# Bilinear sampling: summing over the columns with selector matmuls into quarters of the output partitions, and both weights in one VectorE operation

## The reference, cut to what matters

```python
offsets = lax.conv_general_dilated(x, W, padding='SAME', ...) + b     # 2 numbers per pixel and channel
coords  = off.reshape(bc, -1, 2) + grid                               # one (y, x) per output pixel
c0 = clip(coords[..., 0], 0, w - 1); c1 = clip(coords[..., 1], 0, h - 1)
vals_t = vals_lt + (vals_rt - vals_lt) * f0                           # four gathered neighbours
vals_b = vals_lb + (vals_rb - vals_lb) * f0
mapped = vals_t + (vals_b - vals_t) * f1                              # bilinear value
out = x + mapped
```

## Time and profile before

| | us |
|---|---|
| median of 3 runs | 780.98 (777.89 to 781.43) |
| the profiled execution, its own time | 778.75 |
| its span in the trace | 776.9 |
| PE busy | 642.2 (83%) |
| DVE busy | 680.8 (88%) |
| ACT busy | 534.6 (69%) |
| POOL busy | 453.8 (58%) |

### The profile page before, as it was taken

One profiled execution on the slowest core, in us unless ns is written; L12 is line 12 of the kernel. 1 busy time (PEld: TensorE's weight loads), 2 busy tenths in 40 slices (PEclk: granted clock), 3 DMA queues, 4 the chain that ended last, 5 costly groups with the idle time before them and its releaser, 6 DMA issues.

```text
span 776.9 us, 12483 instructions
## 1 busy us (share of the span) xinstructions
PE 642.2 (83%) x4067; PEld 401.1 (52%) x4067; DVE 680.8 (88%) x958; ACT 534.6 (69%) x660; POOL 453.8 (58%) x282
## 2 busy tenths in 40 slices
PE   7899999999998942686777777777767799999997
PEld 5655547688884310354444444545444553565564
DVE  7899997789976789999889999999999955899997
ACT  2666613789965668677876777868867512899995
POOL 3788873000001165999899999889997911422222
PEclk9999999999999985689897898979987999999999
DMA  2004100440001031000000000000000023100001
GB/s 55 5 12 105 23 1 19 75 96 3 3 3 58 18 80 34 1 1 0 1 0 1 1 0 1 0 1 1 0 2 0 1 52 59 29 0 1 0 0 27
DMA packets 28850, 14.94 MB, mean 19 GB/s; under 512 B 23022, under 2 KB 24942, under 8 KB 28654
## 3 DMA queue, kind: packets, MB, share of 16 engines
q1 hardware_dynamic: 27582, 13.61, 8.2%
q10 hardware_dynamic: 1216, 0.66, 0.4%
HBM read 5.14 MB, written 0.78 MB: 8 GB/s over the span
## 4 chain that ended last, share of the span: by engine, by line
PE 41%; DVE 22%; ACT 6%; issue 6%; POOL 6%; DVEq 0%; POOLq 0%; ACTq 0%
PE ps L572 34%; DVE arena L1374 11%; DVE ps L1042 5%; PE ps L754 4%; POOL arena L1777 4%; PE ps L1007 3%; DVE arena L1042 2%; ACT arena L1725 1%; ACT x L1725 1%; POOL x3t L1777 1%; DVE arena L1317 1%; ACT x1t L1725 1%; DVE arena L1319 1%; POOL xn L1777 1%; ACT arena L1609 0%
## 5 line engine op out<-in xcount | busy, mean ns | idle before, releaser
L572 PE MATMUL ps<-arena 128*64 128x64 f32 (+4 forms) x1944 | 340.6, 341 | 99.1 <-DVE arena L1374 36.3
L572 PEld LDWEIGHTS ps<-arena 128*64 128x64 f32 (+4 forms) x1944 | 138.6, 140 | 216.6 <-issue 83.4
L1777 POOL TENSOR_TENSOR arena<-arena 128x1024 f32<-128x1024 f32 x81 | 188.2, 2335 | 23.4 <-DVE arena L1374 8.5
L1374 DVE TENSOR_TENSOR_SCAN arena<-arena,ps 128x1024 f32<-128x1024 f32 x66 | 150.9, 2287 | 8.6
L1042 DVE TENSOR_TENSOR ps<-arena,ps 128x1024 f32<-128x1024 f32 x75 | 90.9, 1212 | 6.9 <-PE ps L572 6.3
L1758 ACT ACTIVATE arena<-ps,nycol 128x1024 f32<-128x1024 f32 x64 | 70.5, 1101 | 24.9 <-PE ps L572 24.9
L1712 ACT ACTIVATE arena<-arena,a_col 128x1024 f32<-128x1024 f32 x66 | 75.4, 1143 | 16.7 <-DVE arena L1374 16.5
L1894 POOL TENSOR_TENSOR arena<-arena,bmask 128x128 f32<-128x128 f32 x64 | 30.2, 472 | 86.9 <-PE ps L572 75.4
L1374 DVE TENSOR_TENSOR_SCAN arena<-ps,arena 128x1024 f32<-128x1024 f32 x30 | 68.2, 2273 | 4.7 <-POOL arena L1777 4.6
L1609 ACT ACTIVATE arena<-arena 128x256 f32<-128x256 f32 x128 | 60.9, 504 | 11.7 <-DVE arena L1255 7.6
L572 PEld LDWEIGHTS ps<-ident,arena 128*128 128x128 f32 x416 | 58.2, 162 | 15.0 <-issue 6.6
(11 more groups left out here) (206 smaller groups left out, 1178.4 us busy)
## 6 DMA issues: line engine op xcount, KB each, us to landing
arena<-arena SPq DMA_DIRECT2D x54, 64.0 KB
arena<-arena SPq DMA_DIRECT2D x12, 128.0 KB, 3.4
w_conv<-in_c_far SPq DMA_DIRECT2D x1, 1152.0 KB, 5.8
w_conv<-rpb_pad SPq DMA_DIRECT2D x36, 28.0 KB, 1.8
arena<-x SPq DMA_DIRECT2D x12, 64.0 KB, 2.0
arena<-x1t SPq DMA_DIRECT2D x12, 64.0 KB, 2.0
arena<-x3t SPq DMA_DIRECT2D x12, 64.0 KB, 2.0
arena<-arena SPq DMA_DIRECT2D x2, 288.8 KB, 3.7
```

What stands on the lines that cost most here:

```text
L572: return pe.matmul(o, l, r, start=start, stop=stop, **k)
L1374: ve.tensor_tensor_scan(hs_ring[n % RING], decay, add, 0.0, ALU.mult, ALU.add).then_inc(S("scan"), 1)
L1777: return gp.tensor_tensor(o, a, b, ALU.mult)
```

## The change

- `turn4` and the reductions on DVE go. In their place PE sums over the columns: `sum_columns` on PE multiplies a selector (`colsel`, 128 x 32: ones on the 32 partitions of a batch, in that batch's column, zeros elsewhere) with `prod` of each of the 4 groups `t` of a channel step, and writes to partitions 32 t to 32 t + 31 of one bank, 6 + p. Over the eight steps of a half the selector is shifted by one column, and all add up in that one bank, since its other columns are zero. The four matmuls come once for each channel step, 16 times in all. `prod` has 8 buffers in place of 4 so that a whole step can wait.
- After the eighth step of a half, DVE copies the bank (512 wide, `copy_sums`), PE turns it with four transposes (`turn_sums`), and DVE finishes with four small operations that read PSUM (`finish_pair`). For the first half this comes inside step 8 of the loop; POOL finishes nothing any more.
- The hat of y moves from ACT to DVE: `hat4` computes both negated hats in one operation, 1024 wide. ACT keeps the `|d|` alone. The two signs cancel, so `finish` adds where it subtracted.
- PE's loops over the steps are written out; DVE's loop body is two steps long.
- POOL fills `colsel` (a small memset and a copy) before the stage.

```diff
@@ -329,12 +330,13 @@
             pixels = out[b].rearrange("h w c -> (h w) c").rearrange("(k p) c -> p k c", p=P)
             eng.dma_start(pixels[:, blocks], yout[:, blocks, b]).then_inc(S("stored"), 16)
 
-        def finish(eng, p, h):
+        def finish(eng, p, h, b):
+            turned = ps[:, 6 + p, :].rearrange("p (k g a b j) -> p k g a b j", k=4, g=CGRP, a=2, b=2)
             return eng.tensor_tensor(
-                yout[:, 4 * h:4 * h + 4, 2 * p:2 * p + 2].rearrange("p k b (g j) -> p k (b g) j", g=CGRP),
-                x3_row.rearrange("p (k n) -> p k n", k=NBLK)[:, 4 * h:4 * h + 4, DI * p:DI * p + DI]
-                .rearrange("p k (n j) -> p k n j", j=CPER),
-                sampled[:, :, 2 * h:2 * h + 2, :, CPER * p:CPER * p + CPER].rearrange("p k b g j -> p k (b g) j"), ALU.subtract)
+                yout[:, 4 * h:4 * h + 4, 2 * p + b].rearrange("p k (g j) -> p k g j", g=CGRP),
+                x3_row.rearrange("p (k n) -> p k n", k=NBLK)[:, 4 * h:4 * h + 4, DI * p + C * b:DI * p + C * b + C]
+                .rearrange("p k (g j) -> p k g j", g=CGRP),
+                turned[:, :, :, h, b, ::-1], ALU.add)
 
         xn_rows = nc.dram_tensor("xn_rows", (P, C, C), F32, kind="Internal").ap()
         rpb_pad = nc.dram_tensor("rpb_pad", (NH, 13, C, C), F32, kind="Internal").ap()
@@ -989,47 +991,59 @@
             def spread4(j, t):
                 pe.wait_ge(S("abs"), above(j * NT + t - 1))
                 for q in range(2):
-                    last = mm(ps[:, 2 * (t % 2) + q, :], selc[:, t, q], crow[:, j])
+                    last = mm(ps[:, 2 * (t % 2) + q, :], selc[:, t % NT, q], crow[:, j + t // NT])
                 last.then_inc(S("crep"), 1)
 
             def sample(j, t):
                 pe.wait_ge(S("stat"), above(j * NT + (t + 1)))
-                pe.wait_ge(S("hat_y"), above(j * NT + (t + 1)))
+                pe.wait_ge(S("nhat"), above(j * NT + (t + 1)))
                 pe.wait_ge(S("prod"), above(j * NT + t - 1))
                 mm(ps[:, 4 + t % 2, :], xstat[:, t % 2].rearrange("p b x -> p (b x)"),
                    nhat[:, t % NU, 0, :]).then_inc(S("rowmix"), 1)
 
-            def turn4(j, t):
-
-                pe.wait_ge(S("prod"), above(j * NT + (t + 1)))
-                pe.wait_ge(S("summed"), above(j * NT + t - 1))
+            def sum_columns(j, p, at, start=False, stop=False):
+
+                pe.wait_ge(S("prod"), above(j * NT + NT))
+                for t in range(NT):
+                    last = mm(ps[C * t:C * t + C, 6 + p, :], colsel[:, j - CPER * p:j - CPER * p + C], prod[:, at + t],
+                              start=start, stop=stop, skip_group_check=True)
+                last.then_inc(S("colsum"), 1)
+
+            def turn_sums(p):
+
+                pe.wait_ge(S("maps_copied"), p + 1)
                 for c in range(4):
-                    last = pe.transpose(ps[:, 6 + t % 2, P * c:P * c + P], prod[:, t % NU, P * c:P * c + P], ident[:])
-                last.then_inc(S("prod_turned"), 1)
-
-            def map_channels(j, first):
-
-                for t in range(NT):
+                    last = pe.transpose(ps[:, 6 + p, P * c:P * c + P], sampled[:, p, P * c:P * c + P], ident[:])
+                last.then_inc(S("maps_turned"), 1)
+
+            def map_channels(j, p, first=False):
+
+                for t in range(2 * NT):
                     spread4(j, t)
-                    if t >= LAG_MIX or not first:
+                    if t >= LAG_MIX or not (first and p == 0):
                         sample(j, t - LAG_MIX)
-                    if t >= LAG_POS or not first:
-                        if first and t == LAG_POS:
+                    if t == NT - 1:
+                        if not first:
+                            sum_columns(j - 1, p, NT)
+                        elif p:
+                            sum_columns(j - 1, p - 1, NT, stop=True)
+                    if t == NT + 2 and first and p:
+                        turn_sums(p - 1)
+                    if t == 2 * NT - 1:
+                        if first and not p:
                             pe.wait_ge(S("coord"), 2)
-                        turn4(j, t - LAG_POS)
-
-            map_channels(0, True)
-            with pe.Fori(1, CPER) as j:
-                map_channels(j, False)
-            pe.wait_ge(s_ld["rows1"], 16 * 6)
-            with pe.Fori(CPER, NJ) as j:
-                map_channels(j, False)
+                            pe.wait_ge(S("colsel"), 1)
+                        sum_columns(j, p, 0, start=first)
+
+            for p in range(PAIRS):
+                if p:
+                    pe.wait_ge(s_ld["rows1"], 16 * 6)
+                for j in range(CPER * p, CPER * p + CPER, 2):
+                    map_channels(j, p, first=(j == CPER * p))
             for t in range(LAG_MIX):
                 sample(NJ, t - LAG_MIX)
-                turn4(NJ, t - LAG_POS)
-
-            for t in range(LAG_MIX, LAG_POS):
-                turn4(NJ, t - LAG_POS)
+            sum_columns(NJ - 1, 1, NT, stop=True)
+            turn_sums(1)
 
 
         @block.vector
@@ -1441,41 +1455,46 @@
             def hat4(j, t):
 
                 ve.wait_ge(S("abs"), above(j * NT + (t + 1)))
+                ve.wait_ge(S("rowmix"), above(j * NT + (t - NU + 1)))
                 ve.wait_ge(S("prod"), above(j * NT + (t - NU + 1)))
-                ve.tensor_scalar(nhat[:, t % NU, 1], ahat[:, t % NU, 1], 1.0, 1.0, ALU.min, ALU.subtract).then_inc(S("nhat"), 1)
+                ve.tensor_scalar(nhat[:, t % NU], ahat[:, t % NU], 1.0, 1.0, ALU.min, ALU.subtract).then_inc(S("nhat"), 1)
 
             def product(j, t):
                 ve.wait_ge(S("rowmix"), above(j * NT + (t + 1)))
                 ve.wait_ge(S("nhat"), above(j * NT + (t + 1)))
-                ve.wait_ge(S("prod_turned"), above(j * NT + (t - NU + 1)))
-                tt(prod[:, t % NU], ps[:, 4 + t % 2, :], nhat[:, t % NU, 1], ALU.mult).then_inc(S("prod"), 1)
-
-            def sum_columns(j, t):
-
-                ve.wait_ge(S("prod_turned"), above(j * NT + (t + 1)))
-                ve.wait_ge(s_zero, 1)
-                ve.tensor_reduce(sampled[:, :, :, t % NT, bass.ds(j if t >= 0 else j - 1, 1)].rearrange("p k b a -> p k (b a)"),
-                                 ps[:, 6 + t % 2, :].rearrange("p (k b x) -> p k b x", k=4, b=B), AX.X, ALU.add).then_inc(S("summed"), 1)
-
-            def map_channels(j, first):
-                for t in range(NT):
-                    if t >= LAG_MIX or not first:
+                ve.wait_ge(S("colsum"), above(j + t // NT - 1))
+                tt(prod[:, t % NPROD], ps[:, 4 + t % 2, :], nhat[:, t % NU, 1], ALU.mult).then_inc(S("prod"), 1)
+
+            def copy_sums(p):
+                ve.wait_ge(S("colsum"), above(CPER * p + CPER))
+                ve.tensor_copy(sampled[:, p], ps[:, 6 + p, :]).then_inc(S("maps_copied"), 1)
+
+            def finish_pair(p, done):
+                ve.wait_ge(S("x3_row"), 1)
+                ve.wait_ge(S("maps_turned"), p + 1)
+                for h in range(2):
+                    for b in range(2):
+                        last = finish(ve, p, h, b)
+                    last.then_inc(S(done), 1)
+
+            def map_channels(j, p, first=False):
+                for t in range(2 * NT):
+                    if t >= LAG_MIX or not (first and p == 0):
                         product(j, t - LAG_MIX)
                     hat4(j, t)
-                    if t >= LAG_SUM or not first:
-                        sum_columns(j, t - LAG_SUM)
-
-            map_channels(0, True)
-            with ve.Fori(1, NJ) as j:
-                map_channels(j, False)
-            for t in range(-LAG_SUM, 0):
-                if t + LAG_SUM < LAG_MIX:
-                    product(NJ, t + LAG_SUM - LAG_MIX)
-                sum_columns(NJ, t)
-            ve.wait_ge(S("x3_row"), 1)
-            ve.wait_ge(S("summed"), above(NJ * NT))
-            for h in range(2):
-                finish(ve, 1, h).then_inc(S("yout"), 1)
+                    if first and p and t == NT:
+                        copy_sums(p - 1)
+                    if first and p and t == 2 * NT - 1:
+                        finish_pair(p - 1, "yout_first")
+
+            for p in range(PAIRS):
+                map_channels(CPER * p, p, first=True)
+                with ve.Fori(CPER * p + 2, CPER * p + CPER, 2) as j:
+                    map_channels(j, p)
+            for t in range(-LAG_MIX, 0):
+                product(NJ, t)
+            copy_sums(1)
+            finish_pair(1, "yout")
 
 
         @block.scalar
@@ -1754,13 +1773,8 @@
 
                     ac.wait_ge(S("crep"), above(j * NT + (t + 1)))
                     ac.wait_ge(S("nhat"), above(j * NT + (t - NU + 1)))
-                    ac.wait_ge(S("hat_y"), above(j * NT + (t - NU + 1)))
                     ac.activation(ahat[:, t % NU].rearrange("p q n -> p (q n)"), bank2(2 * (t % 2)), ACT.Abs,
```

(4 more changed lines are left out.)

## The result

| | us |
|---|---|
| before, median of 10 runs beside the changed kernel | 778.92 (773.45 to 782.45) |
| changed, median of 10 runs | 773.79 (769.96 to 776.66) |
| ratio, with its 95% interval | 0.9932 [0.9907, 0.9957] |
| forecast | 771.9 (765.5 to 780.5) |
| profiled execution and its span, before | 778.75, 776.9 |

The changed kernel is faster by 5.1 us, with an interval from 3.3 to 7.2. The forecast was 9.1. So the direction and the range hold, and some 4 us of the gain are missing. Two later comparisons of the same two kernels gave 0.9916 [0.9888, 0.9945] and 0.9906 [0.9869, 0.9944].

A forecast was written before the change was run, and what follows sets the result against it. PE was taken to bound the last stage at 1.73 us a unit. Samples 2 to 63 fall from 104.8 to 94.8 us, the end adds 0.9: net -9.1, so 771.9 us against the median, range 765.5 to 780.5.

The forecast's parts named there:

- PE's terms: Steady part on PE: a group costs 1.10 us, a unit falls from 1.73 to 1.29, a four-unit step from 6.92 to 6.26.
- two tiles side by side: Rival on PE's groups: only two quarters run together, a group costs 1.96 us, kernel 785.7 us; chance 0.08.
- three slots: Rival on PE's groups: four tiles need three slots of 0.43, 6.9 us more, kernel 778.8 us; chance 0.08.
- the page's ratio: Trainium skill's 3.07 times for four row tiles, applied to PE's groups: 4 us more than forecast, 775.9 us.
- none: Rival on PE's groups: no quarters run side by side, 41.3 us more, kernel 813 us; chance 0.05.
- Better: Rival on PE's groups: entering and leaving the tiles costs nothing, 3.8 us less, kernel 768.1 us; chance 0.03.
- The bound: Last stage: PE sets the pace at 1.73 us a unit, ACT also needs 1.73, DVE 1.63.
- The middle: Step 8: DVE's copy and four additions, 1.9 us, just hidden; PE's four transposes add 0.44 us uncovered.
- ACT idle for a fifth of the stage: Expected sign in the changed profile: ACT, keeping 1.10 us a unit, idle for about a fifth of the stage.
- The end: From the last sample to the end of the span: 8.6 us in place of 7.7, 0.9 more.
- The start of the stage up to sample 2 hangs on POOL in both: Start of the last stage: sample 2 waits for POOL before and after the change, so no difference; sample 2 near 664.4.
- The late hat: Third rival, DVE: POOL slows the doubled hat to 1.06 us, a unit takes 1.41, kernel 775.4 us; chance 0.12.

The follow-up runs named there:

- e3: Changed kernel with all four matmuls of a group written to one quarter of the partitions, for timing only: 811.27 us in one run.
- e4: Changed kernel with every group of four matmuls issued twice in a row, for timing only: 788.36 us in one run.
- e1: Changed kernel with the hat of y back on ACT, sums over x kept on PE: 780.45 us, ratio 1.001 to the kernel before.
- e2: Kernel before with both hats in one DVE operation, transposes and reductions kept: 782.45 us, ratio 1.0063 to the kernel before.
- the third profile: Changed kernel, unaltered, profiled a third time: 14.15 us from first spread to sample 5, where the first profile had 15.85.
- e7: e6 with POOL's four operations on the coordinates spread among its stationary operands of the first five channel steps: 769.67 us, ratio 0.9891 to the kernel before.
- e8: e6 with the four operations of the coordinates' split moved from POOL to DVE, each behind a hat: 764.22 us, ratio 0.9808 to the kernel before.
- e6: Changed kernel with four buffers for the samples' stationary operands instead of two: 769.7 us, ratio 0.9895 to the kernel before; again 767.1, 0.987.

## Why the prediction was right, and which step was off

The direction and the range hold, and the mechanism on PE is the one that was forecast; the size is 4 us short, for one step that went wrong at the start of the stage.

**PE's terms held.** Group 1.09 for 1.10, unit 1.29, step 6.27 for 6.26, all with one slot of 0.43 for each pass of the four quarters; e3 and e4 show it from both sides. That rules out the three rivals on the group: two tiles side by side (785.7), three slots (778.8, or 775.9 by the page's ratio) and none (813). "Better" is ruled out too, as the change of width is still paid, 0.23.

**The bound was read rightly.** e1 and e2 confirm that the three engines stood close to one another, PE 1.73, ACT 1.73, DVE behind them, and that neither part gains alone. e2 shows one size wrong: the doubled hat, followed by another operation, costs 0.60, not the 0.69 at which its row stands. The prediction was on the safe side with it, and the changed kernel's DVE still had slack, so it cost the forecast nothing. The middle held too: from the group at 718.02 to the next at 724.74 the step with PE's four transposes took 6.72, 0.45 over 6.27 for a forecast of 0.44, and DVE's copy and additions were hidden. One number of the last part was simply miscounted: it expected ACT idle for a fifth of the stage; 4 x 1.11 of 6.27 leave 0.29, and the window shows 31.18 of 44, 0.29 idle.

**The end.** Product 63 starts at 766.45, so sample 63 at about 765.4 (1.06 earlier, as before). From there to 773.7 are 8.3, for a forecast of 8.6. The four additions, priced at 4 x 0.30, took 0.88 together, which is the 0.3.

**The step that failed** is "The start of the stage up to sample 2 hangs on POOL in both", from which I took no difference for the first units. It does hang on POOL in both, and that is why a faster PE and a relieved ACT bring nothing there. But the chain on POOL isn't a constant: the doubled hats run beside its long operations and make them longer, and are made longer by them. From start to start POOL's two tensor_tensor, the cast between them and the first stationary operand take 0.26, 0.26, 0.27 and 0.18 more than before, together the 1.0 us up to sample 2. It is there in all three profiles and in e2. Behind sample 2 the steady price of 1.29 a unit was applied at once, where in the profiled execution TensorE went at half clock for some of these units: 1.8 more. That part varies from 0.1 to 3.2 over the five profiles of this start, so the 1.8 is one draw; had the third profile been the one compared, F to E would have gained 7.8 and not 6.1. In sum -9.1 + 2.8 + 0.2 = -6.1 in the stage, against 5.1 [3.3, 7.2] measured on the medians.

**The late hat**, the third rival, had the right mechanism at the wrong place. It put the collision in the steady part, where a hat would take 1.06 for 0.69 in every unit. There the hats take 0.683 in the mean, and no row of PE waits for DVE. At the start, where POOL's operations are of 1.0 to 2.5 us and meet hats, which read and write SBUF alone, the collision is real and larger than the 0.37 that I took: a hat alone takes 0.68 and beside POOL 1.44 or 2.52 (e7). The 1.60 of the earlier trace rows had shown it, for a hat of half the size; the prediction read that row as a price for the steady part and didn't apply it where it stood. The Trainium skill (GPSIMD Engine Reference, Key points) says that POOL shares its SBUF interfaces with DVE and that operations there in a two-port mode contend. The measured rows agree, and show how much: a hat that starts just behind a POOL operation waits for most of it, 0.76 of 1.03 and 1.84 of 2.12, and POOL's own 2.19 became 2.45 where the hats stand one behind the other.

## What to carry to other kernels

When several engines stand within a few per cent of one pace, cut each unit of work by engine and by start-to-start distance, and expect little from an edit that leaves one of them as it is: here each half of the change alone gave 1.001 and 1.006, and both together 0.993. Price the first units of a stage apart from the steady ones, by who they wait for and what runs beside them. In this kernel a long GpSimd operation cost the SBUF-to-SBUF operation of VectorE beside it most of its own length, and the same work was better placed in VectorE's own gaps (0.9808) than on the engine that looked idle. And compare a start of a few microseconds in more than one profile: the same one took 3.99 to 7.03 here.

## What the runs showed of the hardware

- Four float32 matmuls of 32 output partitions each, 512 columns, with four different moving operands and a shared stationary operand, take one slot of 0.43 per pass, 0.86 in all; into one quarter they take 3.4 (e3). Going from full width to quarters and back costs 0.23 (changed kernel, e4).
- A 128x1024 tensor_scalar on DVE, 0.68 alone, took 1.44 beside a POOL cast of 1.03 and 2.52 beside a POOL tensor_tensor of 2.12 (e7). POOL's operation wasn't slowed there; at the start of the changed kernel, with hats one behind the other, it took 2.45 for 2.19. POOL's work done on DVE took 0.69 and 1.22 (e8).
- Back-to-back DVE operations whose rows read 0.68 started 0.60 apart (e2): a row's duration is more than the operation's share of the engine.
- At the start of this stage TensorE ran at 1.2 GHz for several us in ten of the thirteen profiles (granted clock 0.50), and at 2.4 GHz throughout in e7, e8 and the first of e6. The same three units behind sample 2 took 3.99 to 7.03 in five profiles with the same start, for 3.89 at full clock.
